# A recommendation tower on one NeuronCore: the even tile's lookups and products in another order

## The reference, cut to what matters

```
e = stack([tbl_f[ids[:, f]] for f in range(26)], axis=1)         # 2048 x 26 x 128
combined = concat([dense[:, None, :], e], axis=1)                # 27 vectors a sample
inter = einsum('bnd,bmd->bnm', combined, combined)[:, triu]      # 351 products a sample
h = concat([dense, inter, dense], axis=1)                        # 607
h = max(h @ W_top1 + b_top1, 0)                                  # 512
h = max(h @ W_top2 + b_top2, 0)                                  # 256
y = h @ W_top3                                                   # 1
```

## Time and profile before

| | us |
| --- | --- |
| median of 3 runs | 371.76 |
| lowest, highest | 371.14, 372.31 |
| profiled run | 371.68 |
| its span, first to last instruction | 369.8 |

### The profile page before, as it was taken

One profiled execution on the slowest core, in us unless ns is written; L12 is line 12 of the kernel. 1 busy time (PEld: TensorE's weight loads), 2 busy tenths in 40 slices (PEclk: granted clock), 3 DMA queues, 4 the chain that ended last, 5 costly groups with the idle time before them and its releaser, 6 DMA issues.

```text
span 369.8 us, 13491 instructions
## 1 busy us (share of the span) xinstructions
PE 331.2 (90%) x6048; PEld 295.2 (80%) x6048; DVE 208.4 (56%) x376; ACT 188.2 (51%) x222; POOL 259.1 (70%) x280
## 2 busy tenths in 40 slices
PE   0486759899999999999999989998999989999797
PEld 0476747898899889997899769996889868997676
DVE  3799925792289506980398406980289505960031
ACT  2698643356355664556365554555445552555402
POOL 6777777777777777777777777777777777777100
PEclk9999998999999999999999999999999999999989
DMA  7999527672236512672247322572236512542330
GB/s 178 249 256 206 159 69 236 141 228 56 60 78 171 169 51 62 124 232 60 54 96 194 127 58 54 125 241 51 58 85 158 176 52 53 110 111 59 77 47 14
DMA packets 49332, 44.24 MB, mean 120 GB/s; under 512 B 33359, under 2 KB 39094, under 8 KB 49274
## 3 DMA queue, kind: packets, MB, share of 16 engines
q1 hardware_dynamic: 39166, 25.36, 27.4%
q0 software_dynamic: 8704, 17.84, 18.0%
q10 hardware_dynamic: 1404, 0.17, 0.3%
HBM read 37.91 MB, written 5.44 MB: 117 GB/s over the span
## 4 chain that ended last, share of the span: by engine, by line
PE 78%; DMA 8%; POOL 4%; issue 4%; SPq 2%; ACT 2%; DVE 0%; DVEq 0%
PE banks L449 37%; PE banks L472 13%; PE mlp L492 8%; PE moved L431 8%; PE mlp L502 7%; DMA hidden<-in_tbl_dram 6%; POOL rows L404 4%; DMA rows<-in_tbl_dram,ids_sb 3%; SPq L253 2%; PE banks L538 1%; PE mlp L514 1%; PE banks L552 1%; ACT vectors L866 1%; ACT vectors L849 1%; PE mlp L538 1%
## 5 line engine op out<-in xcount | busy, mean ns | idle before, releaser
L404 POOL DMA_INDIRECT rows<-in_tbl_dram,ids_sb x272 | 258.1, 949 | 83.9 <-issue 80.2
L711 DVE TENSOR_TENSOR masks<-hot_ids,row_of 125x512 fp32r<-125x512 int32 (+1 forms) x336 | 186.4, 619 | 59.9 <-PE banks L449 51.6
L449 PE MATMUL banks<-masks,high 125*128 125x256 f32 x592 | 152.4, 296 | 16.7 <-DVE low L698 16.7
L449 PE MATMUL banks<-masks,low 125*128 125x256 f32 x592 | 147.2, 287 | 0.0
L449 PEld LDWEIGHTS banks<-masks,high 125*128 125x128 f32 x592 | 115.6, 195 | 17.7 <-issue 14.6
L449 PEld LDWEIGHTS banks<-masks,low 125*128 125x128 f32 x592 | 115.9, 196 | 0.0
L866 ACT ACTIVATE vectors<-moved 128x512 f32<-128x512 f32 (+1 forms) x79 | 86.5, 1094 | 22.6 <-PE moved L431 22.6
L849 ACT ACTIVATE vectors<-banks 128x512 f32<-128x512 f32 (+1 forms) x40 | 44.4, 1110 | 70.4 <-PE banks L449 70.4
L472 PEld LDWEIGHTS banks<-vectors 128*27 128x27 f32 x4096 | 45.6, 104 | 22.6 <-issue 14.8
L472 PE MATMUL banks<-vectors 128*27 128x27 f32 x4096 | 56.3, 193 | 4.7 <-issue 3.7
L431 PE MATMUL moved<-identity,rows 128*128 128x128 f32 x271 | 45.0, 281 | 14.1 <-ACT vectors L866 6.4
(11 more groups left out here) (49 smaller groups left out, 65.4 us busy)
## 6 DMA issues: line engine op xcount, KB each, us to landing
hot_ids<-in_ids_of_field_dram SPq DMA_DIRECT2D x32, 256.0 KB, 4.7
rows<-in_tbl_dram,ids_sb POOLq DMA_INDIRECT x272
features<-scratch SPq DMA_DIRECT2D x7, 351.0 KB
scratch<-products SPq DMA_DIRECT2D x56, 42.2 KB
scratch<-products SPq DMA_DIRECT2D x28, 81.2 KB
w_sb<-in_tbl_dram SPq DMA_DIRECT2D x3, 448.0 KB
hot_ids<-in_ids_of_field_dram SPq DMA_DIRECT2D x8, 128.0 KB
dense_sb<-in_dense_dram SPq DMA_DIRECT2D x8, 128.0 KB, 5.3
```

The lines of the kernel that those rows point to most:

```text
L404: pool.indirect_dma_start(rows[:, (tile * TILE_ROWS + v) % RING, :], None, tables[f][:, :], bass.IndirectOffsetOnAxis(ap=ids_sb[:, tile, f ...
L449: last = nc.tensor.matmul(banks[:, j % BANKS, m * CHUNK:(m + 1) * CHUNK], part[:, part_of(j * PAIR + m, k), :], masks[:, mask % MASK_RING, ...
L711: nc.vector.tensor_tensor(masks[:, mask % MASK_RING, 0:size], hot_ids[0:PART_ROWS, n % ID_RING, 0:size], row_of[0:PART_ROWS, row:row + 1]. ...
```

## The change

Nothing is computed otherwise; TensorE, ACT, DVE and SP get another order.

- A chunk now begins lookup 1 of the next chunk behind the visits of steps 2 and 3: parts 0 to 3 there, parts 4 to 7 after turn 0 of the next even tile.
- Turn 4 of the even tile stands after six of the ten parts of lookup 4, where it stood after all of them.
- Lookup 0 of the next chunk moves ahead, in two pieces, around turn 3 of the odd tile.
- Half 1 of the second layer is split, two matmuls before step 2 and two between its visits.
- The order is the same from chunk 1 on (`second_chunk` is gone).
- In the last chunk step 0 and all layers of the chunk before come earlier, and the first two of four parts of half 0's first layer stand between steps 2 and 3.
- DVE makes the masks of lookup 1 before it places the dense vectors; SP stores y of chunk 6 before the second half's writes.

The diff of the order, first TensorE's:

```diff
@@ TensorE, end()
                 b = ALL_TILES - 1
-                first_layer(LAST - 1, 0)
-                multiply(LAST, 0, (0,))
+                multiply(LAST, 0)
                 turn(b, 0)
+                multiply(LAST, 1, (0,))
                 first_layer(LAST - 1, 1)
-                multiply(LAST, 0, (1,))
+                multiply(LAST, 1, (1,))
                 turn(b, 1)
-                multiply(LAST, 1, (0,))
                 first_layer(LAST - 1, 2)
-                multiply(LAST, 1, (1,))
+                first_layer(LAST - 1, 3)
                 turn(b, 2)
-                first_layer(LAST - 1, 3)
-                second_layer(LAST - 1, 0, range(0, 2))
+                second_layer(LAST - 1, 0)
+                second_layer(LAST - 1, 1)
                 turn(b, 3)
-                second_layer(LAST - 1, 0, range(2, MTILES1))
+                last_layer(LAST - 1)
                 turn(b, 4)
-                second_layer(LAST - 1, 1, range(0, 2))
                 multiply(LAST, 2)
-                multiply(LAST, 3)
-                second_layer(LAST - 1, 1, range(2, MTILES1))
-                last_layer(LAST - 1)
                 first_of_half(0, 0, every)
                 first_of_half(0, 1, every)
+                multiply(LAST, 3)
                 first_of_half(0, 2, every)
                 first_of_half(0, 3, every)
@@ TensorE, first_chunk()
                 turn(1, 1)
-                multiply(0, 0)
+                multiply(0, 0, (0,))
                 turn(1, 2)
-                multiply(0, 1)
+                multiply(0, 0, (1,))
                 turn(1, 3)
+                multiply(0, 1, (0,))
+                look_up(1, 0, range(0, 3))
+                multiply(0, 1, (1,))
+                look_up(1, 0, range(3, PARTS[0]))
                 turn(1, 4)
-                multiply(0, 2, (0,))
-                look_up(1, 0, range(0, 3))
-                multiply(0, 2, (1,))
-                look_up(1, 0, range(3, 5))
-                multiply(0, 3, (0,))
-                look_up(1, 0, range(5, PARTS[0]))
-                multiply(0, 3, (1,))
+                products_of_second_tile(0)
+
+            def products_of_second_tile(i):
+                multiply(i, 2, (0,))
+                second_layer(i - 1, 1, range(2, MTILES1))
+                multiply(i, 2, (1,))
+                look_up(i + 1, 1, range(0, 2))
+                multiply(i, 3, (0,))
+                look_up(i + 1, 1, range(2, 4))
+                multiply(i, 3, (1,))
@@ TensorE, chunk(i)
                 turn(a, 0)
-                look_up(i, 1)
+                look_up(i, 1, range(4, PARTS[1]))
                 last_layer(i - 2)
...
                 turn(a, 3)
-                look_up(i, 4)
+                look_up(i, 4, range(0, 6))
                 turn(a, 4)
+                look_up(i, 4, range(6, PARTS[4]))
                 first_layer(i - 1, 0)
+                if i == LAST:
+                    return
                 multiply(i, 0, (0,))
                 turn(b, 0)
                 first_layer(i - 1, 1)
                 multiply(i, 0, (1,))
+                first_layer(i - 1, 2)
                 turn(b, 1)
-                first_layer(i - 1, 2)
                 multiply(i, 1, (0,))
-                turn(b, 2)
                 first_layer(i - 1, 3)
-                turn(b, 3)
                 multiply(i, 1, (1,))
                 second_layer(i - 1, 0)
+                turn(b, 2)
+                look_up(i + 1, 0, range(0, 6))
+                turn(b, 3)
+                look_up(i + 1, 0, range(6, PARTS[0]))
                 turn(b, 4)
-                second_layer(i - 1, 1)
-                multiply(i, 2, (0,))
-                look_up(i + 1, 0, range(0, 3))
-                multiply(i, 2, (1,))
-                look_up(i + 1, 0, range(3, 5))
-                multiply(i, 3, (0,))
-                look_up(i + 1, 0, range(5, PARTS[0]))
-                multiply(i, 3, (1,))
+                second_layer(i - 1, 1, range(0, 2))
+                products_of_second_tile(i)
@@ DVE, end() and the loop over chunks
-                keep_last_row()
-                keep_step(LAST, 3)
                 keep_second()
                 keep_y()
+                keep_last_row()
                 first_of_half(0)
                 first_of_half(1)
+                keep_step(LAST, 3)
...
                 make_masks(i, 0)
+                make_masks(i, 1)
                 place_dense(i)
-                make_masks(i, 1)
@@ ACT, chunk(i) and what was end_of_chunk(i)
                 keep_pair(i, 3)
                 keep_batch(a, 3)
+                keep_batch(a, 4)
                 keep_pair(i, 4)
-                keep_batch(a, 4)
...
                 keep_step(i, 1)
                 keep_second(i - 1, 0)
+                keep_batch(b, 2)
+                keep_batch(b, 3)
+                keep_pair(i + 1, 0)
                 keep_batch(b, 4)
                 keep_second(i - 1, 1)
                 keep_step(i, 2)
-                keep_pair(i + 1, 0)
                 keep_step(i, 3)
@@ SP
             write_last(0)
             load_last(0)
+            store_y(LAST - 1)
             write_last(1)
-            store_y(LAST - 1)
             load_last(1)
```

More of the change, by code:

```diff
@@ L964, in first_chunk @@
                 keep_batch(1, 1)
+                keep_batch(1, 2)
                 keep_step(0, 0)
-                keep_batch(1, 2)
+                keep_batch(1, 3)
                 keep_step(0, 1)
-                keep_batch(1, 3)
+                keep_pair(1, 0)
                 keep_batch(1, 4)
                 keep_step(0, 2)
-                keep_pair(1, 0)
                 keep_step(0, 3)
-            def second_chunk():
-                keep_batch(2, 0)
-                keep_pair(1, 1)
-                keep_batch(2, 1)
-                keep_pair(1, 2)
-                keep_batch(2, 2)
-                keep_pair(1, 3)
-                keep_batch(2, 3)
-                keep_pair(1, 4)
-                keep_batch(2, 4)
-                end_of_chunk(1)
             def chunk(i):
-                a = TILES * i
+                a, b = TILES * i, TILES * i + 1
                 keep_batch(a, 0)
@@ L995, in chunk @@
                 keep_batch(a, 3)
+                keep_batch(a, 4)
                 keep_pair(i, 4)
-                keep_batch(a, 4)
-                if i < LAST:
-                    end_of_chunk(i)
-            def end_of_chunk(i):
-                b = TILES * i + 1
                 keep_first(i - 1, 0)
+                if i == LAST:
+                    return
                 keep_batch(b, 0)
@@ L1021, in end_of_last @@
                 b = ALL_TILES - 1
-                keep_first(LAST - 1, 0)
+                keep_step(LAST, 0)
                 keep_batch(b, 0)
                 keep_first(LAST - 1, 1)
-                keep_step(LAST, 0)
+                keep_step(LAST, 1)
                 keep_batch(b, 1)
                 keep_first(LAST - 1, 2)
-                keep_step(LAST, 1)
+                keep_first(LAST - 1, 3)
                 keep_batch(b, 2)
-                keep_first(LAST - 1, 3)
+                keep_second(LAST - 1, 0)
                 keep_batch(b, 3)
-                keep_second(LAST - 1, 0)
             first_chunk()
-            second_chunk()
-            for i in range(2, CHUNKS):
+            for i in range(1, CHUNKS):
                 chunk(i)
```

24 lines of the change are left out of this document (3 added, 21 removed).

## The result

| | us |
| --- | --- |
| before, median of 4 runs (lowest, highest) | 371.68 (371.14, 372.31) |
| changed, median of 4 runs (lowest, highest) | 376.23 (375.08, 376.57) |
| ratio, 95% interval | 1.0094, 1.0055 to 1.0133 |
| profiled run of the changed kernel, and its span | 375.93, 374.1 |

The changed kernel is slower by 0.6 to 1.3%. The middle of that interval is 3.5 us; the two medians lie 4.6 us apart, near its upper end. The forecast was 377.6 us, 1.4 above the median; the range of 371.7 to 380.5 held it, and slower, at 0.79, was right. Here and in the experiments, ratios leave out runs in a slower state (among them one of the kernel before at 772.29 us), which the medians contain.

The account below looks back on a forecast made before the run. Gathers (42.5 us a chunk) and a 23.6 us tail bound the kernel; 1.83 us of new costs a chunk use up TensorE's 2 us spare. Chunk 1 at 63.4, plus 254.3, 33.1 and the tail: span 375.7, time 377.6, range 371.7 to 380.5.

Parts of the forecast that it names:

- The two turns: Turn 4 of each tile waits for ScalarE's copy of turn 3: 0.76 us (even) and 0.67 us (odd) a chunk.
- The first visit of step 2: TensorE waits there for the copy of turn 4, queued behind lookup 0's copy: 0.25 us a chunk, bounds 0 to 0.4.
- the switches: Lookups and second layer cut into more pieces cost TensorE 0.15 us a chunk, bounds 0 to 0.4.
- Chunk 0: Earlier pauses and slow clock go or shrink, so chunk 1 starts at 63.4 instead of 65.7 us; bounds 62.4 to 66.
- the pause would go: In chunk 0, TensorE's 1.97 us pause without a releaser at 63.6 us was to go or shrink.
- The last chunk: From its turn 0 to the last tile's turn 4: 33.1 us instead of 31.8, with the last turn at 350.8.
- The tail: After the last turn: step 3 kept at 357.8, load used at 366.4, then 7.8 us plus 1.5 for a lower clock.
- ride on the gathers: Rival, chance 0.20: TensorE's waits are smaller or repaid, last turn at 345.3, time 370.6 to 372.1 us.
- the waits were whole and not half: Rival, chance 0.15: only half the waits, some 1 us a chunk plus overhead; last turn about 347, time 373 to 375.
- the third rival: Chance 0.10: TensorE pauses, starved of instructions, in every chunk; 0.5 us each gives 381 us, 1.96 about 389.

Follow-up runs that it names:

- e1: Changed kernel with turn 4 of each tile in its own PSUM bank and the masks' row numbers moved to SBUF; 385.28 us (1.0298 of the kernel before).
- e12: e7's body and changed end, but steps 2 and 3 back to back, all four parts of half 0's first layer behind them; 369.96 us (0.9961).
- e9: Changed kernel with the last chunk of the kernel before on all engines; 373.14 us (1.0042 of the kernel before).
- e10: Kernel before with the changed last chunk alone; 375.80 us (1.0119 of the kernel before).
- e8: Kernel before with only the even tile's turn 4 moved, to stand after six parts of lookup 4; 371.46 us (1.0000 of the kernel before).
- e3: Changed kernel with even turn 4 after all of lookup 4 again and lookup 0 cut 4 + 4 around odd turn 3; 373.61 us (1.0052).
- e5: Changed kernel with only the even tile's turn 4 put back after all of lookup 4; 376.01 us (1.0119 of the kernel before).
- e6: Changed kernel with only lookup 0 cut 4 + 4 instead of 6 + 2 around the odd tile's turn 3; 376.49 us (1.0128 of the kernel before).
- e7: e3 with ScalarE's copy of the odd turn 4 put ahead of its copy of lookup 0; 372.62 us (1.0037 of the kernel before).

## Why the prediction was right, step by step

**The two turns.** 0.76 and 0.67 us were predicted, 0.74 and 0.64 measured against the distances that were called due (0.74 and 0.60 against those of e1). The way there holds: the end of ScalarE's copy plus 0.14 us.

**The first visit of step 2 and the switches.** 0.25 and 0.15 a chunk were predicted; from the odd turn 4 to the visit are 1.18 us (225.86 to 227.04), 0.16 more than the prediction gave to the work between, and of the switches nothing is to be seen. From turn 0 of chunk 1 (64.62) to that of the last chunk (316.18) are 251.6 us, so 41.9 a chunk instead of the 42.3 predicted. Two errors meet in this. Three pauses of 0.33, 0.44 and 1.05 us without a releaser are in it, which the sum did not have. Without them and the 1.38 us of waits a chunk, 241.5 us are left for TensorE's own work, where the prediction took 243.3 and added 2.4 for the first visit and the switches. Of those two terms nothing is to be seen, and why the own work is even 1.8 us shorter than before is open.

**Chunk 0.** 63.4 was predicted for its end and 64.62 measured. The step that failed is that the pause would go: it is still there, 1.76 us before 59.78, and the clock was at 0.50 after it. This error of 1.2 us takes back a part of the 2.7 us by which the chunks were put too long: turn 0 of the last chunk was predicted at 317.7 and came at 316.18.

**The last chunk.** 33.1 us to the last turn were predicted, 33.5 measured, with a pause of 1.13 us before 337.19 that the sum did not have. (The rows that turn 0 of this chunk needs end with the 242nd gather, not the 241st, so they can be there at 307.8 and not at 306.5; nothing rests on it.) The last turn was put at 350.8 and came at 349.66.

**The tail.** Turn to step 3 kept: 6.95 predicted, 6.39 measured; the pause between the steps went as foreseen, and it came back (2.25 us) where e12 put the steps back to back again. From there to the use of the load: 8.6 predicted, 8.80 measured. The idle time and the lower clock came as described, and from the load's use to the end are 9.27 us, against 7.8 + 1.5 = 9.3 predicted. That the whole came within 1.4 us is in part luck, since the errors of the body have opposite signs; the direction is not, since the waits that made it are there one by one.

**The rivals.** TensorE did not ride on the gathers (its last turn came 5.2 us after it could), the waits were whole and not half, and it was not starved in every chunk, though four pauses, 2.95 us in all from 85 to 338 us, show that the third rival was real in kind.

**What the prediction lacked** is how the parts lean on each other. It summed body and end. e9 and e10 show 1.7 and 4.4 us for a whole of 3.5 to 4.6. The kernel before had spare time on TensorE, and e8 shows it taking up 3.4 us of waits at no cost. e3, e5 and e6 show the other side: a wait taken away uncovers the next one (step 2's copy, the pairs from the scratch), so that 4.4 us of waits were worth 1.8 over six chunks in e5, and nothing clear in its time. In this kernel a sum of removed or added waits was an upper bound and no forecast.

## What to carry to other kernels

When a wait on one engine is moved or removed, list what arrives next at that place, with its slack: here the slack of the pairs was between 0.04 and 2.1 us, and decided e5. Put the small copy that the next step needs ahead of the large one that nobody waits for: e7, which also sets both turns back, is 3.6 us under the changed kernel, and e3, which has the turns alone, still waits 3.7 us at step 2. And keep independent TensorE work for a wait at the very end instead of using it to fill a pause ahead of it: here the pause cost no more than the work put into it, while the idle array met a lower clock in the last matmuls.

## What the runs showed of the hardware

**The array's clock in the tail.** After 4.6 to 5.0 us of idle the last matmuls began at a granted clock of 0.50, or had it soon after, and the stretch from the landing to the end took 9.4 to 10.4 us. After 2.44 us of idle (e12) the clock was 1.00, and it took 7.9; in the kernel before, whose TensorE had work until the load was there, it was 1.00 as well, and it took 8.3. A shorter idle time is not safe by itself: in e1 it was 2.96 us, the clock still fell, 1.5 us after the work had begun again, and the stretch took 9.5 us:

```profile
377.20:380.40 3.20, 3.20 (x17) 3.20 (x16) 0.00 (x0) 1.10 (x3) 0.00 (x0) 0.50 0.02 5
```

Each of these is one run's trace.

**DVE and the gathers.** Moving a one-column operand of DVE's masks from PSUM to SBUF slowed GpSimd's gathers from 946 to 992 ns on the mean, and the kernel by some 8 us.

**Pauses without a releaser.** TensorE's pauses came just behind the fetch of one 16 KB block on the instruction queue q8, in the changed kernel too: this is that queue from 334.2 to 336 us (packets, MB, share):

```profile
q8 instruction: 1, 0.02, 5.1%
```

TensorE's next record behind it:

```profile
337.19 0.42 PE L472 MATMUL banks<-vectors 128*27 128x27 f32 x32 [1.13 <-issue]
```

By the trace's packets the fetch ran from 334.45 to 335.93, and TensorE's last record ahead of the pause began at 335.87. In e9 the products of steps 2 and 3 stand back to back; a fetch ran from 351.94 to 353.37, and a pause of 2.45 us followed 238 records. In the changed kernel, with larger matmuls between the steps, a fetch ran from 352.15 to 353.11 without a pause. What the times have in common is where a pause ends:

| kernel | fetch ended | pause | TensorE went on | behind the fetch |
| --- | --- | --- | --- | --- |
| before | 64.36 | 1.97 | 65.85 | 1.49 |
| before | 350.02 | 1.96 | 351.44 | 1.42 |
| changed | 58.32 | 1.76 | 59.78 | 1.46 |
| changed | 169.53 | 1.05 | 170.97 | 1.44 |
| changed | 335.93 | 1.13 | 337.19 | 1.26 |
| e12 | 348.26 | 2.25 | 349.65 | 1.39 |

In the fourteen traces there are 62 pauses of over 0.25 us without a releaser behind the first 48.5 us, and every one of them ends 1.2 to 1.6 us after such a fetch has ended, though there are only 48 such fetches in a trace. (One pause of 0.38 us in each trace, which ends between 44 and 48.2 us, is of another kind.) This fits a TensorE that has run out of instructions, mostly in dense small matmuls, as the prediction read the earlier trace rows, and speaks against a mere coincidence. That q8 carries TensorE's instructions is taken from this, and no run took a fetch away, so the cause is not shown by an experiment.
